# Expert loop of a mixture-of-experts block: one TensorE signal a tile, turns in pairs three tiles ahead, results copied out three tiles behind

## The reference, cut to what matters

```python
ys = _geglu(xf @ Ws1 + bs1) @ Ws2 + bs2            # shared, HS = 256
logits = (xf @ Wr + br) / TAU                      # E = 12 experts
top_val, top_idx = jax.lax.top_k(logits, 2)
top_w = jax.nn.softmax(top_val, axis=-1)
h = jnp.einsum('nd,edh->enh', xf, We1) + be1[:, None, :]   # 128 -> 2 * HR, HR = 384
act = _geglu(h)                                    # a * gelu(g)
yE = jnp.einsum('enh,ehd->end', act, We2) + be2[:, None, :]  # 384 -> 128
yr = jnp.einsum('end,ne->nd', yE, w)               # weighted sum of the two chosen
return (ys + yr).reshape(B, T, Dm)
```

## Time and profile before

| | us |
|---|---|
| time of the runs, median of 3 | 1334.11 (1333.97 to 1338.37) |
| profiled execution, span of core 0 | 1379.4 |
| PE busy in it | 1188.3 (86%) |
| DVE busy | 924.9 (67%) |
| ACT busy | 848.1 (61%) |
| POOL busy | 783.9 (57%) |
| mean granted clock of TensorE | 0.947 |

### The profile page before, as it was taken

The page is one execution under the profiler, slowest core; times in us unless marked ns, Lnnn a source line. Parts: engine busy times, 40 slices in busy tenths (PEclk is TensorE's granted clock), DMA queues, the critical chain, the costliest instruction groups (busy, mean ns, idle before and its releaser), DMA issues.

```text
span 1379.4 us, 36586 instructions
## 1 busy us (share of the span) xinstructions
PE 1188.3 (86%) x12757; PEld 888.2 (64%) x12758; DVE 924.9 (67%) x2489; ACT 848.1 (61%) x2486; POOL 783.9 (57%) x700
## 2 busy tenths in 40 slices
PE   5899898998889999799989899897878958868884
PEld 2667676776645555467668567684768835558783
DVE  6998669986846777698866988688322366643233
ACT  3999769997435555489985899843344533323443
POOL 6787358883644352388834878444666511266653
PEclk9999999999979999899999999998898989779997
DMA  7011100111000000001110001131655520145564
GB/s 219 17 25 25 30 13 17 25 25 29 15 2 3 4 3 3 2 13 27 26 28 16 9 21 31 30 77 33 182 170 168 152 62 0 31 125 168 177 175 121
DMA packets 70226, 79.26 MB, mean 57 GB/s; under 512 B 25191, under 2 KB 50598, under 8 KB 69926
## 3 DMA queue, kind: packets, MB, share of 16 engines
q1 hardware_dynamic: 64421, 65.49, 16.9%
q0 software_dynamic: 5632, 11.55, 3.1%
HBM read 55.52 MB, written 8.91 MB: 47 GB/s over the span
## 4 chain that ended last, share of the span: by engine, by line
PE 60%; DVE 11%; ACT 10%; issue 6%; DMA 5%; POOL 2%; SPq 1%; POOLq 1%; another core or an unknown queue 1%; ACTq 0%; DVEq 0%; PEldq 0%; PEld 0%
PE bank L1842 10%; PE bank L912 5%; PE bank L1856 5%; ACT pB L791 5%; DMA arena<-arena 4%; PE bank L633 3%; PE bank L596 3%; PE bank L1511 3%; PE bank L924 3%; PE bank L555 3%; PE bank L1532 3%; PE bank L541 3%; PE bank L608 2%; PE bank L1543 2%; PE bank L547 2%
## 5 line engine op out<-in xcount | busy, mean ns | idle before, releaser
L2103 DVE SCALAR_TENSOR_TENSOR act_b<-bank,vec,gl 128x128 f32<-128x128 f32 x264 | 76.6, 345 | 182.5 <-PE bank L1842 65.3
L860 POOL TENSOR_TENSOR rn<-ss,mhalf 128x16 f32<-128x16 f32 x64 | 187.2, 2925 | 6.9
L1925 ACT ACTIVATE gl<-bank,vec 128x128 f32<-128x128 f32 x264 | 77.7, 365 | 120.9 <-PE bank L1842 90.7
L1842 PE MATMUL bank<-arena 128*128 128x128 f32 x1056 | 146.5, 293 | 4.5 <-DVE act_b L2103 1.6
L1842 PEld LDWEIGHTS bank<-arena 128*128 128x128 f32 x1056 | 136.3, 206 | 10.9 <-issue 5.9
L2178 POOL DMA_INDIRECT arena<-u_rows,inv_u x88 | 86.1, 979 | 71.5 <-remote 31.2
L791 ACT ACTIVATE pA<-bank,nb,rn 128x128 f32<-128x128 f32 x256 | 113.5, 484 | 3.6 <-DVE nb L722 3.6
L791 ACT ACTIVATE pB<-bank,nb,rn 128x128 f32<-128x128 f32 x256 | 113.3, 478 | 1.7 <-DVE nb L722 1.7
L2184 POOL DMA_INDIRECT y_rows<-stg,inv_u x88 | 86.5, 983 | 42.9 <-ACT stg L1932 21.9
L846 POOL TENSOR_TENSOR arena<-arena 128x512 f32<-128x512 f32 x64 | 81.6, 1275 | 46.3 <-DVE nb L722 35.7
L853 POOL TENSOR_TENSOR arena<-arena 128x512 f32<-128x512 f32 x64 | 81.3, 1271 | 43.0 <-DVE arena L685 16.3
(11 more groups left out here) (336 smaller groups left out, 3141.1 us busy)
## 6 DMA issues: line engine op xcount, KB each, us to landing
arena<-in_L_ffn_We SPq DMA_DIRECT2D x88, 384.0 KB
arena<-arena SPq DMA_DIRECT2D x64, 128.0 KB, 2.3
arena<-in_L_ffn_We SPq DMA_DIRECT2D x3, 768.0 KB, 7.4
arena<-U SPq DMA_DIRECT2D x32, 64.0 KB
u_rows<-U SPq DMA_DIRECT2D x2, 1024.0 KB, 5.2
U<-y_rows SPq DMA_DIRECT2D x8, 256.0 KB, 4.1
uT<-y_rows SPq DMA_DIRECT2D x8, 256.0 KB, 4.8
arena<-U SPq DMA_DIRECT2D x32, 63.5 KB
```

Source lines behind the costliest of these rows:

```text
L860: pool.tensor_tensor(rn[:, q % 4, :, :], ss[:, 1, :].rearrange("p (a h) -> p a h", a=2), mhalf[:, :].rearrange("p (a h) -> p a h", a=2), A ...
L1842: m = pe.matmul(bank[q % 2][:, j * P:(j + 1) * P], we1[q][:, half * HR + j * P:half * HR + (j + 1) * P], xT[:, q, :], start=True, stop=True)
```

## The change

The four counters `x_ps`, `x_up`, `x_dn` of TensorE become one, `x_pe`, which is raised once a tile, by the last record of the up projection. Since TensorE completes in order, that event also says that all earlier turns and down projections are done; three helper functions give the count to wait for. Only the first three turns, two of them alone and one pair, and the last three down projections have signals of their own. The turns of two tiles are done together after every odd tile, for tiles `n + 3` and `n + 4`, in two places of `XIN`, and one 128x256 copy takes both. ScalarE copies the result of tile `n - 3` ahead of the GeLU of tile `n`. VectorE's wait for `x_dn` goes: the up projection's event covers it.

```diff
--- before.py
+++ after.py
...
@@ -1770,11 +1770,23 @@
         def x_loads(k0, buf):
             return k0 * (NXT // XG + (buf < NXT % XG))
 
+        X_EVENTS = NXT + 6
+        X_TURNS = NXT // 2 + 1
+
+        def turn_seen(k0, n):
+            return k0 * X_EVENTS + (n + 1 if n < 2 else 4 if n < 4 else n + 2 - n % 2)
+
+        def up_seen(k0, n):
+            return k0 * X_EVENTS + (n + 4 if n else 3)
+
+        def down_seen(k0, n):
+            return k0 * X_EVENTS + n + 7
+
         def expert(eng, n):
             return eng.value_load(te[0:1, n:n + 1], min_val=0, max_val=E - 1)
 
         def mx_pe(pe, k0):
-            kc, base = k0 * NCH, k0 * NXT
+            kc, base, turns = k0 * NCH, k0 * NXT, k0 * X_TURNS
 
             def up(c, g):
                 if c:
@@ -1823,16 +1835,22 @@
                 return pe.value_load(te[0:1, bass.ds(n, 1)], min_val=0, max_val=E - 1)
 
             def x_turn(i, o, q):
-                n, buf = 8 * i + 4 * o + q, 4 * o + q
+                buf = 4 * o + q
                 pe.wait_ge(LD_X[buf], 16 * (x_loads(k0, buf) + i + 1))
-                if not (isinstance(i, int) and n == 0):
-                    pe.wait_ge(s.x_T, base + n)
-                pe.transpose(XIN[:, 0:P], xg[:, buf, :], ident[:, :]).then_inc(s.x_ps, 1)
+                return pe.transpose(XIN[:, q % 2 * P:(q % 2 + 1) * P], xg[:, buf, :], ident[:, :])
+
+            def x_pair(i, o, q):
+                pe.wait_ge(s.x_T, turns + 4 * i + 2 * o + q // 2 + 1)
+                x_turn(i, o, q)
+                return x_turn(i, o, q + 1)
 
             def x_up(i, o, q):
                 n = 8 * i + 4 * o + q
                 pe.wait_ge((s.ld_e0, s.ld_e1, s.ld_e2, s.ld_e3)[q], 16 * (NXG * k0 + 2 * i + o + 1))
-                pe.wait_ge(s.x_T, base + n + 1)
+                if isinstance(i, int) and n < 2:
+                    pe.wait_ge(s.x_T, turns + n + 1)
+                elif q % 2 == 0:
+                    pe.wait_ge(s.x_T, turns + 4 * i + 2 * o + q // 2 + 2)
                 if isinstance(i, int) and n < 2:
                     pe.wait_ge(s.s_a, 2 * (kc + NCH))
                 else:
@@ -1842,7 +1860,7 @@
                         m = pe.matmul(bank[q % 2][:, j * P:(j + 1) * P],
                                       we1[q][:, half * HR + j * P:half * HR + (j + 1) * P], xT[:, q, :],
                                       start=True, stop=True)
-                    m.then_inc(s.x_up, 1)
+                m.then_inc(s.x_pe, 1)
 
             def x_down(i, o, q):
                 n = 8 * i + 4 * o + q
@@ -1855,7 +1873,8 @@
                 for j in range(3):
                     m = pe.matmul(XY[q % 2][:, 0:D], XACT[q][:, j * P:(j + 1) * P],
                                   we2[:, bass.ds(e * HR + j * D, D)], start=(j == 0), stop=(j == 2))
-                m.then_inc(s.x_dn, 1)
+                if isinstance(i, int) and n >= NXT - 3:
+                    m.then_inc(s.x_pe, 1)
 
             def group(i, o):
                 for q in range(4):
@@ -1867,9 +1886,11 @@
                         x_down(i, 0, q + 2)
                     elif not (isinstance(i, int) and i == 0):
                         x_down(i - 1, 1, q + 2)
-                    if not (isinstance(i, int) and n + 2 >= NXT):
-                        k = 4 * o + q + 2
-                        x_turn(i + k // 8, k % 8 // 4, k % 4)
+                    if isinstance(i, int) and n == 0:
+                        x_pair(0, 0, 2).then_inc(s.x_pe, 1)
+                    elif q % 2 and not (isinstance(i, int) and n + 3 >= NXT):
+                        k = 4 * o + q + 3
+                        x_pair(i + k // 8, k % 8 // 4, k % 4)
                     if isinstance(i, int) and n in SH_AT:
                         shared(SH_AT[n])
 
@@ -1887,8 +1908,9 @@
                 ring(m)
             pe.wait_ge(s.ld_w, 16 * (2 * DEPTH + N_EW))
             pe.wait_ge(s.r_tab, 3 * k0 + 2)
-            x_turn(0, 0, 0)
-            x_turn(0, 0, 1)
+            x_turn(0, 0, 0).then_inc(s.x_pe, 1)
+            pe.wait_ge(s.x_T, turns + 1)
+            x_turn(0, 0, 1).then_inc(s.x_pe, 1)
             for i in range(OCT):
                 group(i, 0)
                 group(i, 1)
@@ -1910,23 +1932,23 @@
                 act.activation(sh_a[:, c, g, :], sh_up(g)[0][:, :], ACT.Identity, bias=vec[:, V_BS1 + g:V_BS1 + g + 1])\
                     .then_inc(s.s_a, 1)
 
-            def x_out(n):
-                act.wait_ge(s.x_ps, base + n + 1)
-                if n > 3:
-                    act.wait_ge(s.x_up, 2 * (base + n - 3))
-                act.activation(xT[:, n % 4, :], XIN[:, 0:P], ACT.Copy).then_inc(s.x_T, 1)
+            def x_out(n, w):
+                act.wait_ge(s.x_pe, turn_seen(k0, n + w - 1))
+                act.activation(xT[:, n % 4:n % 4 + w, :],
+                               XIN[:, n % 2 * P:(n % 2 + w) * P].rearrange("p (w k) -> p w k", w=w), ACT.Copy)\
+                    .then_inc(s.x_T, 1)
 
             def gelu(n, e):
                 if n > 1:
                     act.wait_ge(s.x_act, 3 * (base + n - 1))
-                act.wait_ge(s.x_up, 2 * (base + n) + 1)
+                act.wait_ge(s.x_pe, up_seen(k0, n))
                 for j in range(3):
                     js = slice(j * P, (j + 1) * P)
                     act.activation(XGELU[n % 2][:, js], XG_BANK[n % 2][:, js], ACT.Gelu,
                                    bias=vec[:, bass.ds(e * 6 + (3 + j), 1)]).then_inc(s.x_gl, 1)
 
             def y_out(n):
-                act.wait_ge(s.x_dn, base + n + 1)
+                act.wait_ge(s.x_pe, down_seen(k0, n))
                 if n + k0 * NXT > 3:
                     act.wait_ge((s.st_y0, s.st_y1, s.st_y2, s.st_y3)[n % 4], 16 * (NXG * k0 + n // 4))
                 act.activation(yb[:, n % 4, :], XY[n % 2][:, 0:D], ACT.Copy).then_inc(s.x_y, 1)
@@ -1939,15 +1961,15 @@
                     act.wait_ge(s.r_wps, k0 + 1)
                     act.activation(wT[:, :], W_BANK[:, :], ACT.Copy).then_inc(s.r_wT, 1)
             act.wait_ge(s.r_tab, 3 * k0 + 2)
-            x_out(0)
-            x_out(1)
-            for n in range(NXT + 2):
+            x_out(0, 1)
+            x_out(1, 1)
+            for n in range(NXT + 3):
+                if n > 2:
+                    y_out(n - 3)
                 if n < NXT:
                     gelu(n, expert(act, n))
-                if n > 1:
-                    y_out(n - 2)
-                if n + 2 < NXT:
-                    x_out(n + 2)
+                if n % 2 == 0 and n + 2 < NXT:
+                    x_out(n + 2, 2)
 
         R_PLACES = 32
         R_STEPS = 44
@@ -2094,9 +2116,7 @@
             assert taken[0] == (k0 + 1) * R_STEPS, taken
 
             def act_in(n, e):
-                if n > 3:
-                    dve.wait_ge(s.x_dn, base + n - 3)
-                dve.wait_ge(s.x_up, 2 * (base + n) + 2)
+                dve.wait_ge(s.x_pe, up_seen(k0, n))
                 for j in range(3):
                     js = slice(j * P, (j + 1) * P)
                     dve.wait_ge(s.x_gl, 3 * (base + n) + j + 1)
@@ -2174,7 +2194,7 @@
 
             def gather(n):
                 if n >= XG:
-                    pool.wait_ge(s.x_ps, base + n - XG + 1)
+                    pool.wait_ge(s.x_pe, turn_seen(k0, n - XG))
                 pool.indirect_dma_start(xg[:, n % XG, :], None, u_rows[:, :],
                                         bass.IndirectOffsetOnAxis(ap=inv_u[:, 0, n:n + 1], axis=0))\
                     .then_inc(LD_X[n % XG], 16)
@@ -2223,7 +2243,7 @@
             sp.wait_ge(s.r_tab, 3 * k0 + 2)
             for n in range(NXT):
                 if n >= WB:
-                    sp.wait_ge(s.x_up, 2 * (base + n - WB + 1))
+                    sp.wait_ge(s.x_pe, up_seen(k0, n - WB))
                 e = expert(sp, n)
                 sp.dma_start(we1[n % WB], a["L1_ffn_We1"][bass.ds(e, 1), :, :].rearrange("o k n -> k (o n)"))\
                     .then_inc((s.ld_e0, s.ld_e1, s.ld_e2, s.ld_e3)[n % WB], 16)
```

More of the change, by code:

```diff
@@ L52 @@
 a_out alpha_ready r_lg r_self r_m12 r_pool r_both r_cum r_wps r_wT s_up s_act s_dn s_tmp ld_x0 ld_x1 st_y0 st_y1
-x_ps x_T x_gl x_act x_dn x_y gat0 gat1 x_sum passed ld_x2 ld_x3 ld_e0 ld_e1 ld_e2 ld_e3 r_w s_a uT_ready x_up
+x_T x_gl x_act x_y gat0 gat1 x_sum passed ld_x2 ld_x3 ld_e0 ld_e1 ld_e2 ld_e3 r_w s_a uT_ready x_pe
 r_tab h_ld n_gps n_gate n_kps n_k n_neg n_exp n_kf n_qps n_qf n_vps n_v n_att n_am n_num n_den n_rec n_o
```

## The result

The changed kernel takes 1339.69 us (median of 20 runs, 1335.51 to 1348.23); the kernel before, timed beside it, 1334.04. The ratio is 1.0041, interval [1.0029, 1.0052]: slower by some 5.5 us where 18 us faster were forecast. One of the 20 runs of the kernel before took 1532.72 us and is a slow one that the ratio leaves out. The profiled execution took 1337.43 us, its span 1335.6.

The account below looks back on a forecast made before the run. It took TensorE's signals, seen late behind GpSimd's runs of indirect DMAs, as the bound, GpSimd second. Terms -15 - 3 + 1 and 1 for the clock gave -18 us, from 1334 to 1316; range 1298 to 1341.

Parts of the forecast that it names:

- I carry the 18 us over whole: 1316: Whole kernel: the 18 us expected off the profiled 1379.4 us span was taken unreduced from the timed median 1334.1.
- 15 + 3 us: Both expert loops: fewer late signals save 15 us over the middle tiles and 3 us at the loops' starts.
- the 36 that the prediction took for its bound: Upper bound on the signals' gain: GpSimd's whole rest in both loops, 15.7 + 15.2 + about 5 us.
- Rival (b): Loop middles: the lateness belongs to the profiled execution only, so timed runs gain little, 1335 us; chance 0.12.
- 2.5 us for the single one, 2.8 us a tile: Loop middles: a tile's single signal is seen 2.5 us late, so a tile takes 2.8 us against 3.04.
- Rival (a): Loop middles: the two-tile beat stays, signals passing only after GpSimd's run, 6.2 us per two tiles; 1335 us, chance 0.20.
- Without lateness it is hidden: GeLU after the whole up projection: starts 0.67 us later, but 2.9 us are available and the chain needs 1.7.
- rival (c): Restarts after stalls: the later GeLU behind a copy lengthens each, 0.4 us for 44 restarts, 18 us; 1352 us, chance 0.20.
- a tail of 0.5 us a loop: Copies out three behind: four instead of three scatters in a row at each loop's end, 1 us in all.
- Turns in pairs: Turning two tiles together: one copy of 0.39 us instead of two of 0.29, on an idle engine, worth nothing.
- the lead of the gathers: Gathers get 5 to 6 tiles of lead instead of 8, 11 us or more, judged enough to cover a gather.
- The microsecond for the clock: Loop middles: 1 us gained from less slow clock, shown there as 0.94 and 0.92 against 1.00.

Follow-up runs that it names:

- e1: The kernel before, unchanged, profiled and timed again: ratio 1.0007 to the kernel before, span 1335.8 us.
- e5: The new kernel unchanged, in the series where the kernel before takes 1381.72 us: 1385.5 us, ratio 1.0031.
- e10: The kernel before with only the GeLU waiting for the whole up projection, signals not late: ratio 1.0004.
- e7: The kernel before with only the GeLU waiting for the whole up projection, signals late: ratio 1.003.
- e9: The kernel before with only the copy out three tiles behind and ahead of the GeLU, signals not late: ratio 0.9997.
- e2: The new kernel with copies out two tiles behind, after the GeLU, on a signal of every down projection: ratio 1.0003 to the kernel before.
- e11: The new kernel with copies out two behind, after the GeLU, every down projection signalled, timed a second time: ratio 1.0015 to the kernel before.
- e18: The new kernel with two scatters after gathers 18, 22 and 26, so scatters then lie 9 gathers behind instead of 12: ratio 1.0047 to the kernel before.
- e4: The new kernel with scatters 13 instead of 12 behind the gathers: ratio 1.0025 to the kernel before.
- e8: The kernel before with two scatters after gathers 18, 22 and 26, scatters then 9 instead of 12 behind, signals late: ratio 1.0003.

## Why the prediction was wrong

**What bounds the kernel, and the sum.** Read rightly for the execution shown, but not for the ones timed. The step that failed is "I carry the 18 us over whole: 1316". Its 15 + 3 us were the price of late signals, and at 1334 us there are none: e1 has GpSimd idle 6.9 / 5.8 us a loop, where the rest was put at 15.7 and 15.2 for the middles alone. All that was left to win there was under 13 us of the 36 that the prediction took for its bound. Rival (b) had the arithmetic for it, two middles 55 us shorter, near the gap of 45; the loops in fact differ by 44.3. Its 0.12 was too little: a gap of 45 us between the profile and the runs is evidence about the very stretch on which the argument stood.

**Signals: 2.5 us for the single one, 2.8 us a tile.** Wrong where it could be tried. At the late level (e5) a tile takes 3.15 us, not 2.8, and the ratio is 1.0031. So this term fails there too. The 2.5 us came from one signal that got out in the midst of a run; what holds in the middle of e5 is the restart behind GpSimd's run of four, which gives 4 x 1.28 + 1.1 = 6.2 us, measured 6.3. Rival (a) had the mechanism.

**GeLU after the whole up projection.** "Without lateness it is hidden": e10 (1.0004 [0.9985, 1.0022]) is in accord. With lateness it is rival (c): it costs 0.3% (e7), 4 us of the 18 that the rival priced. The rival's condition, that TensorE and not GpSimd's run closes the beat, was not met in e5, which may be why; no run shows it.

**Copies out three behind.** The order is free, as costed (e9). The error was in what a copy waits for. Its row in the sum was a tail of 0.5 us a loop; the wait for the up projection of tile n + 3 was not priced at all. By the two groups of runs it costs about 3 us, 0.2%. The 11.1 us ahead of the copies are not its price, since most of them were ahead of the GeLU before.

**Turns in pairs, the lead of the gathers, the clock.** The turns in pairs were never tried alone; with them, and the copies signalled early, e2 and e11 stand at 1.0003 and 1.0015. The lead was enough at 12 behind (no wait of TensorE for a gather in the middle), and not at 9 (e18). The microsecond for the clock had no place to come from: it is 1.00 in the middle of the first loop in both kernels.

**What stays open.** The loss of 5.5 us is not split to the end. The copies' wait carries about 3 us of it; the late GeLU has at most a fifth of a per cent at the fast level (e10); single parts are of the size of their intervals. The new kernel itself was timed only once at that level, and its 1.0041 is above every variant of it with 12 or 13 tiles between gathers and scatters, so part of the rest may be the series. Why the same kernel runs at 1336 us in some series and at 1381 in another, with TensorE's signals late behind GpSimd's DMAs, was not found; nothing in the kernel differs between them. The record gives the series e1 to e4 (1336.44) and e5 to e8 (1381.72) the same chip number, 6, so if the number names one chip, the level is not a trait of the chip.

## What to carry to other kernels

If the profiled execution and the timed runs lie apart by more than the effect in question, find the stretch in which they differ before costing anything in it, and get a profile at the level of the runs. Merging signals gained nothing that shows here, and each consumer then waits for the last of the merged events: price each one's new wait by the queue behind it, here the scatters on GpSimd. A wait that moves from one instruction to the next on the same engine is no cost: add up both before blaming either. And where an engine's queue of DMAs is the bound, try its order: issuing the scatters three tiles sooner gave 0.5% beside the old signals and nothing in the new kernel. Last, look at how far two profiles of one kernel lie apart before reading a few microseconds out of two profiles.

## What the hardware showed that was not expected

The same kernel ran at 1336.44, 1335.03, 1335.59 and 1337.28 us (medians of four series) and at 1381.72 in a fifth. At the level of late signals TensorE's finished work is seen only 0.9 to 1.1 us after a run of GpSimd's indirect DMAs ends, whether it gives four signals a tile or one; at the fast level there is no such delay beside the same DMAs. In the new kernel's profile there:

```profile
1009.38 1.50 PE L1860 MATMUL bank<-arena 128*128 128x128 f32 x12
...
1009.96 0.97 POOL L2198 DMA_INDIRECT arena<-u_rows,inv_u  x1 [0.30 <-issue]
...
1010.92 0.28 ACT L1954 ACTIVATE stg<-bank 128x128 f32<-128x128 f32 x1 [0.19 <-PE bank L1860]
```

The up projection ends at 9.38 + 1.50 = 1010.88, and the copy that waits for it starts 0.04 us later, with GpSimd in the midst of its run. The granted clock does not explain it: in the middle of the loop it is 0.98 in e5 and 1.00 in the new kernel's profile at the fast level, with 581 against 742 records of TensorE in 93 us.
